# One gather per edge step into fixed buffers, with constant addresses and waits, in both layers of a graph convolution

## The reference

```python
def _gcn_layer(x, src, dst, norm, W, b, num_nodes):
    xw = x @ W
    msg = xw[src] * norm[:, None]          # norm = dis[src] * dis[dst]
    out = segment_sum(msg, dst, num_segments=num_nodes)
    return out + b
...
xn = _layernorm(x)
h = elu(_gcn_layer(xn, ..., W1, b1)); h = elu(_gcn_layer(h, ..., W2, b2))
x = x + h + mix(xn)                        # linear attention, 8 heads
x = x + ffn(_layernorm(x))                 # top 2 of 8 experts, 256 -> 1024 -> 256
```

## Time and profile before

| | us |
|---|---|
| time before, median of 3 runs | 3345.3 |
| lowest and highest of them | 3343.86, 3346.88 |
| span of the profiled execution | 3317.0 |
| PE busy in it | 2369.2 (71%) |
| POOL busy | 1965.4 (59%) |
| DVE busy | 1747.8 (53%) |
| ACT busy | 619.3 (19%) |

### The profile page before, as it was taken

The page is one execution under the profiler, slowest core; times in us unless marked ns, Lnnn a source line. Parts: engine busy times, 40 slices in busy tenths (PEclk is TensorE's granted clock), DMA queues, the critical chain, the costliest instruction groups (busy, mean ns, idle before and its releaser), DMA issues. The chain is left out here.

```text
span 3317.0 us, 45225 instructions
## 1 busy us (share of the span) xinstructions
PE 2369.2 (71%) x10847; PEld 1754.6 (53%) x10847; DVE 1747.8 (53%) x4268; ACT 619.3 (19%) x1318; POOL 1965.4 (59%) x2107
## 2 busy tenths in 40 slices
PE   3366766666776678356666566666669499999998
PEld 2244444444444446234444344434448399999997
DVE  6144444444444456245444455555556666676666
ACT  2000000000000005000000011110006444444443
POOL 1566666666666653766666666666644155555554
PEclk9777888888877879677777877787789599999999
DMA  6333333333333322444444445444431455555551
GB/s 170 114 94 88 93 90 90 92 91 92 89 93 88 89 77 80 122 138 139 141 147 140 140 146 148 146 145 144 144 92 63 170 185 148 148 148 151 148 149 20
DMA packets 177902, 397.25 MB, mean 120 GB/s; under 512 B 42393, under 2 KB 96570, under 8 KB 169514
## 3 DMA queue, kind: packets, MB, share of 16 engines
q0 software_dynamic: 96800, 233.29, 26.7%
q1 hardware_dynamic: 50926, 103.38, 8.7%
q10 hardware_dynamic: 30012, 58.67, 5.2%
HBM read 322.87 MB, written 75.01 MB: 120 GB/s over the span
## 5 line engine op out<-in xcount | busy, mean ns | idle before, releaser
L644 POOL DMA_INDIRECT rows<-rows_layer,srcs x1564 | 1538.3, 984 | 762.3 <-issue 382.0
L705 PE MATMUL l_bank<-rows,sel 128*128 x3332 | 1191.5, 487 | 638.8 <-issue 246.1
L695 DVE TENSOR_TENSOR acc<-acc,l_bank 128x256 f32 x1666 | 698.9, 419 | 1233.1 <-remote 546.7
L705 PEld LDWEIGHTS l_bank<-rows,sel 128*128 128x128 f32 x3332 | 700.3, 235 | 1013.3 <-issue 482.7
L1638 PE MATMUL ps_y<-whl,hhi 128*128 128x512 f32 x896 | 320.8, 398 | 0.0
L1594 POOL DMA_INDIRECT out<-ys,g_sum x112 | 179.9, 1606 | 200.5 <-DVE ys L1550 175.2
L673 DVE TENSOR_TENSOR sel<-iota_n,dloc 128x512 f32<-128x512 f32 x418 | 286.4, 686 | 20.1 <-issue 20.1
L1509 ACT ACTIVATE hr<-ffn_bank,vec 128x256 f32<-128x256 f32 x448 | 212.7, 475 | 374.2 <-PE ffn_bank L1450 336.8
L1448 PE MATMUL ffn_bank<-xh,whl 128*128 128x256 f32 x896 | 252.2, 281 | 2.4 <-DVE xl L1524 2.4
L1449 PE MATMUL ffn_bank<-xl,whl 128*128 128x256 f32 x896 | 252.0, 281 | 0.0
L1450 PE MATMUL ffn_bank<-xh,whl 128*128 128x256 f32 x896 | 251.9, 281 | 0.0
(11 more groups left out here) (273 smaller groups left out, 2208.3 us busy)
## 6 DMA issues: line engine op xcount, KB each, us to landing
whl<-w_hi SPq DMA_DIRECT2D x32, 1024.0 KB
whl<-w_lo SPq DMA_DIRECT2D x32, 1024.0 KB
rows<-rows_layer,srcs POOLq DMA_INDIRECT x1564
w_qkv<-wide ACTq DMA_DIRECT2D x49, 335.0 KB
w_hi<-whi ACTq DMA_DIRECT2D x49, 335.0 KB
w_lo<-wlo ACTq DMA_DIRECT2D x49, 335.0 KB
rows_layer<-acc SPq DMA_DIRECT2D x25, 256.0 KB, 2.1
rows_x<-acc SPq DMA_DIRECT2D x7, 910.0 KB
```

The costliest lines, as they stand in the source:

```text
L644: pool.indirect_dma_start(rows[:, (n + 1) % ROWS, :], None, table[layer], bass.IndirectOffsetOnAxis(ap=srcs[:, n:n + 1], axis=0)).then_inc ...
L695: v.tensor_tensor(to, to, step_bank(s), ALU.add).wait_op(sem(f"summed{layer}"), s + 1, "sem-ge").then_inc(sem(f"added{layer}"), 1)
L705: t.matmul(step_bank(s), sel[:, s % SELS, :], rows_flat[:, bass.ds(slot * D, D)], start=True, stop=True).wait_op(sem(f"here{layer}"), t.to ...
```

## The change

Gathers, matmuls and adds now go by the same number, the step. `srcs` holds an index column for each of the 833 steps instead of 782 tiles, so a tile that two blocks share is gathered twice. Step s writes and reads slot s % 32, PE waits for the landing of its own step by a constant, and POOL waits by a constant for PE's sum 32 steps earlier. `tiles_here`, `steps_until_free` and `tiles_of` go; SP has nothing to do in the layers. DVE's part of a step is unchanged, its register loads (`blocks_of`) too. In the preparation the sources are gathered by `t_i` on POOL like the destinations, seven indirect DMAs behind the seven, in place of SP's two plain ones, and one set of word pairs is stored instead of three.

```diff
-        srcs = sb(steps_ctx, "srcs", [P, ET], I32)
+        srcs = sb(steps_ctx, "srcs", [P, SG * P], I32)
...
-                    sp.wait_ge(sem("copy_s"), 32)
-                    sp.dma_start(rows_i[:, 1, 0:SG - 1, :], e_src_rows[0:full, :].rearrange("(g p) w -> p g w", p=P)
-                                 ).then_inc(sem("rows_s"), 16)
-                    sp.dma_start(rows_i[0:ET - full, 1, SG - 1, :], e_src_rows[full:ET, :]).then_inc(sem("rows_s"), 16)
-                    sp.wait_ge(sem("word_i"), 6)
+                    sp.wait_ge(sem("word_i"), 2)
                     with nc.allow_non_contiguous_dma("small"):
-                        for k in range(3):
-                            sp.dma_start(tab_d[k, :, :].rearrange("(g p) w -> p g w", p=P), word_i[:, k, :, :]
-                                         ).then_inc(sem("word_d"), 16)
+                        sp.dma_start(tab_d[0, :, :].rearrange("(g p) w -> p g w", p=P), word_i[:, :, :]
+                                     ).then_inc(sem("word_d"), 16)
...
                         pool.indirect_dma_start(rows_i[:, 0, g, :], None, e_dst_rows, at).then_inc(sem("rows_d"), 16)
+                    pool.wait_ge(sem("copy_s"), 32)
+                    for g in range(SG):
+                        at = bass.IndirectOffsetOnAxis(ap=t_i[:, g:g + 1], axis=0)
+                        pool.indirect_dma_start(rows_i[:, 1, g, :], None, e_src_rows, at).then_inc(sem("rows_s"), 16)
                     pool.wait_ge(sem("counted"), 2)
...
                     for k in range(2):
-                        v.tensor_scalar(word_i[:, 0, :, k], t_i[:, :], 1.0, None, ALU.add).then_inc(sem("word_i"), 1)
-                        v.tensor_scalar(word_i[:, 1, :, k], b_s[:, :], float(D), None, ALU.mult).then_inc(sem("word_i"), 1)
-                        v.tensor_copy(word_i[:, 2, :, k], tb[:, :]).then_inc(sem("word_i"), 1)
+                        v.tensor_scalar(word_i[:, :, k], b_s[:, :], float(D), None, ALU.mult).then_inc(sem("word_i"), 1)
...
         def gathers(pool, layer, rows):
-            for n in range(ET):
-                if n >= ROWS:
-                    pool.wait_ge(sem(f"freed{layer}"), n - ROWS + 1)
-                pool.indirect_dma_start(rows[:, (n + 1) % ROWS, :], None, table[layer],
-                                        bass.IndirectOffsetOnAxis(ap=srcs[:, n:n + 1], axis=0)
-                                        ).then_inc(sem(f"slot_{n % ROWS}"), 16)
+            for s in range(STEPS):
+                if s >= ROWS:
+                    pool.wait_ge(sem(f"summed{layer}"), s - ROWS + 1)
+                pool.indirect_dma_start(rows[:, s % ROWS, :], None, table[layer],
+                                        bass.IndirectOffsetOnAxis(ap=srcs[:, s:s + 1], axis=0)
+                                        ).then_inc(sem(f"slot_{s % ROWS}"), 16)
+        def landed(layer, s):
+            return (s // ROWS + 1 + layer * -(-(STEPS - s % ROWS) // ROWS)) * 16
...
-        def step_sum(t, layer, s, here):
-            slot = t.snap(here & (ROWS - 1))
-            t.to_reg(slot)
+        def step_sum(t, layer, s, rows):
             if s < PSB:
                 t.wait_ge(sem(f"selected{layer}"), s // FOUR + 1)
             else:
                 t.wait_ge(sem(f"added{layer}"), s - PSB + 1)
-            t.matmul(step_bank(s), sel[:, s % SELS, :], rows_flat[:, bass.ds(slot * D, D)], start=True, stop=True
-                     ).wait_op(sem(f"here{layer}"), t.to_reg(here), "sem-ge").then_inc(sem(f"summed{layer}"), 1)
+            t.matmul(step_bank(s), sel[:, s % SELS, :], rows[:, s % ROWS, :], start=True, stop=True
+                     ).wait_op(sem(f"slot_{s % ROWS}"), landed(layer, s), "sem-ge").then_inc(sem(f"summed{layer}"), 1)
...
-                @block.sync
-                def _(sp):
-                    tiles_here(sp, 0)
```

More of the change, by code:

```diff
@@ L36 @@
 TURN = 16
-BEHIND, FREED_AT = 16, 8
-assert ROWS > BEHIND and ROWS & (ROWS - 1) == 0 and PAD_DST + NT < 1 << 16 and BLOCKS * D < 1 << 16 and ET < 1 << 16
+assert PAD_DST + NT < 1 << 16 and BLOCKS * D < 1 << 16 and ET < 1 << 16
 HEADS, HD = 8, 32
@@ L106, in gps_layer @@
     e_src = dram("edges_src", [ET * P, 1], I32)
-    tab_d = dram("step_words", [3, SG * P, 2], U16)
+    tab_d = dram("step_words", [1, SG * P, 2], U16)
     table = [dram(f"rows_layer{i}", [n * P, D], F32) for i, n in enumerate((NT, 2 * PAIRS))]
@@ L152, in gps_layer @@
         dloc = sb(steps_ctx, "dloc", [P, SG * P])
-        srcs = sb(steps_ctx, "srcs", [P, ET], I32)
-        words = sb(steps_ctx, "words", [3, SG * P, 2], U16)
+        srcs = sb(steps_ctx, "srcs", [P, SG * P], I32)
+        words = sb(steps_ctx, "words", [1, SG * P, 2], U16)
         ctx_q = sb(steps_ctx, "ctx_q", [P, KC, D])
@@ L364, in gps_layer @@
             b_128 = sb(ph, "b_128", [P, SG])
-            word_i = sb(ph, "word_i", [P, 3, SG, 2], U16)
+            word_i = sb(ph, "word_i", [P, SG, 2], U16)
             rows_i = sb(ph, "rows_i", [P, 2, SG, P], I32)
@@ L403, in _ @@
                 def _(sp):
-                    full = ET // P * P
-                    sp.wait_ge(sem("copy_s"), 32)
-                    sp.dma_start(rows_i[:, 1, 0:SG - 1, :], e_src_rows[0:full, :].rearrange("(g p) w -> p g w", p=P)
-                                 ).then_inc(sem("rows_s"), 16)
-                    sp.dma_start(rows_i[0:ET - full, 1, SG - 1, :], e_src_rows[full:ET, :]).then_inc(sem("rows_s"), 16)
-                    sp.wait_ge(sem("word_i"), 6)
+                    sp.wait_ge(sem("word_i"), 2)
                     with nc.allow_non_contiguous_dma("small"):
-                        for k in range(3):
-                            sp.dma_start(tab_d[k, :, :].rearrange("(g p) w -> p g w", p=P), word_i[:, k, :, :]
-                                         ).then_inc(sem("word_d"), 16)
+                        sp.dma_start(tab_d[0, :, :].rearrange("(g p) w -> p g w", p=P), word_i[:, :, :]
+                                     ).then_inc(sem("word_d"), 16)
                     sp.wait_ge(sem("rows_d"), SG * 16)
@@ L418, in _ @@
                     sp.dma_start(node[0:TAIL, NT - 1, :], x[(NT - 1) * P:N, :]).then_inc(sem("x_last"), 16)
-                    sp.wait_ge(sem("word_d"), 48)
+                    sp.wait_ge(sem("word_d"), 16)
                     sp.dma_start(words[:, :, :], tab_d).then_inc(sem("words"), 16)
@@ L571, in _ @@
                             ins.then_inc(sem("rows_t"), 1)
-                    t.wait_ge(sem("rows_f"), 2)
+                    t.wait_ge(sem("rows_f"), 1)
                     for g in range(SG):
-                        n = min(P, ET - g * P)
-                        ins = t.transpose(ps_src[:, g * P:g * P + n], rows_f[0:n, g, :], ident[0:n, 0:n])
+                        ins = t.transpose(ps_src[:, g * P:(g + 1) * P], rows_f[:, g, :], ident[:, :])
                         if g % 4 == 3 or g == SG - 1:
@@ L610, in _ @@
                     a.activation(hi_b[:, :], hi_i[:, :], ACT.Copy).then_inc(sem("hi_b"), 1)
[L611 to L615, removed]
+                    a.wait_ge(sem("rows_s"), SG * 16)
+                    a.activation(rows_f[:, :, :], rows_i[:, 1, :, :], ACT.Copy).then_inc(sem("rows_f"), 1)
+                    for j, (lo, hi) in enumerate(ROW_COLS):
                         a.wait_ge(sem("rows_t"), j + 3)
@@ L679, in blocks_of @@
             _, regs = nc.values_load_multi_w_load_instructions(
-                words[1:2, s:min(s + LOADED, STEPS), 0], engines=(DVE_ENGINE,), min_val=0, max_val=(BLOCKS - 1) * D,
+                words[0:1, s:min(s + LOADED, STEPS), 0], engines=(DVE_ENGINE,), min_val=0, max_val=(BLOCKS - 1) * D,
                 skip_runtime_bounds_check_because="a step's tile is one of the step's number or less, by less than the blocks")
-            return list(regs)
-        def tiles_of(s):
-            _, regs = nc.values_load_multi_w_load_instructions(
-                words[0:1, s:min(s + LOADED, STEPS), 0], engines=(PE_ENGINE,), min_val=1, max_val=ET,
-                skip_runtime_bounds_check_because="a count of tiles, 1 to ET")
             return list(regs)
@@ L720, in vector_steps, with tensor_steps @@
                     between(s // TURN, s % TURN)
-        def tensor_steps(t, layer, between):
-            tiles = tiles_of(0)
+        def tensor_steps(t, layer, rows, between):
             for s in range(STEPS):
-                step_sum(t, layer, s, tiles[s])
-                if s % LOADED == 1 and s + LOADED - 1 < STEPS:
-                    tiles.extend(tiles_of(s + LOADED - 1))
+                step_sum(t, layer, s, rows)
                 if s < NT * TURN:
@@ L741, in gps_layer @@
             rows = sb(ph, "rows0", [P, ROWS, D])
-            rows_flat = rows[:, :, :].rearrange("p r d -> p (r d)")
             sel = sb(ph, "sel0", [P, SELS, P])
@@ L841, in between @@
                             ins.then_inc(sem("m_kv"), 1)
-                    tensor_steps(t, 0, between)
```

(6 more changed lines are left out.)

## The result

The changed kernel takes 3439.1 us (3437.7 to 3440.1, 4 runs) against 3345.5 us, a ratio of 1.0278 with the interval 1.0263 to 1.0292: 93.6 us slower. The forecast was 3420 us, slower by 74.5.

A forecast was written before the change was run, and what follows sets the result against it. PE's late completions after gathers in a row, not POOL's own work, were taken to bound the layers. 2 x (40.8 - 4.9) + 2.7 = +74.5 on 3345.3 gave 3419.8, say 3420 us; range 3162 to 3491.

The forecast's parts named there:

- case A: Whole kernel: the jam stays and 51 more gathers a layer lengthen it, 3382 to 3491 us; chance 0.52.
- the jam: Both layers: after some ten microseconds of gathers in a row, PE's completions come late until POOL pauses.
- The signs: Profile after: 833 gathers 1.39 to 1.45 us apart, POOL idle for PE, layers about 36 us longer, preparation wait near 31.4.
- signs of being wrong: Profile after: gathers 1.29 us apart without waits, a mean gather above 986 ns, or preparation moved over 10 us.
- The base of p: Layer 0 before: gathers start 1.450 us apart in the 3317.0 us span, with 28.3 us lying around it.
- What p becomes: Both layers: gather spacing falls from 1.450 to 1.41 us through PE's lighter step, making +40.8 us a layer.
- The drain: After each layer's last gather: at most 32 steps of 0.786 us remain, 25.2 instead of 30.1 us, -4.9 a layer.
- The preparation: Before layer 0: seven more gathers delay DVE's release from 22.64 to 31.4, costing +2.7 us.
- The bound of -6.1: Preparation: if the gathered destinations land as early as DVE can take them, its 6.11 us idle time goes.
- PE's loads, waits and SP's part at nothing: Layers: PE's register loads and waits and SP's removed work get no term of their own.
- Rival B: Layers: PE's and SP's register and semaphore work causes the jam, so it goes and POOL binds, 3162 us; chance 0.28.
- Case C: Layers: the jam partly eases through PE's lighter step, gathers 1.35 to 1.387 us apart, 3320 to 3382 us; chance 0.20.

The follow-up runs named there:

- run 9: Kernel before, with SP's three word-pair stores moved behind its loads of x: 3336.8 us against 3341.6, ratio 0.9987, on a chip with the jam.
- run 10: Changed kernel fetching 64 rows of 1 KB instead of 128 from each layer's 33rd gather on: 3444.4 us against 3341.6, on a chip with the jam.
- run 8: Changed kernel with three stores of word pairs and their four small DVE operations put back: 3138.5 us, 6.8 above the changed kernel on that chip.
- run 12: Kernel before with the three stores late and a ring of 16 slots, SP 8 tiles behind: 3010.5 us against 3015.1, ratio 0.9985.
- runs 2 and 11: Changed kernel with PE's register loads and operations put back, on two chips without the jam: 3135.9 us (ratio 1.0398) and 3132.9 us (1.0382).
- run 5: Changed kernel as it is, on a chip without the jam: 3131.7 us against 3014.4 for the kernel before, ratio 1.0384.
- run 3: Changed kernel with only the first 32 gathers of each layer, all other work kept: 2474.8 us, on a chip without the jam.
- run 1: Kernel before, unchanged and profiled again, on a chip without the jam: 3016.3 us, with a span of 3014.4.

## Why the prediction was right, and where its steps were off

**The side and the case.** The forecast case A happened: the jam stayed, 51 gathers a layer came on top. The time of 3439 lies inside A's own range. That the price is the number of gathers was shown by leaving 51 of them out (run 6), on a chip without the jam. With the jam it rests on the two traces, which have the same steps and nearly the same price of a gather; no run left gathers out there.

**The signs.** Three of those named came true: 833 gathers a layer, 1.444 us apart, with POOL waiting for PE for 832 x (1.444 - 1.286) = 131 us a layer; DVE's add standing 7.68 us at the end of a run of gathers; and all behind layer 1 as long as it was. Two did not: the layers grew by 63 us and not 36, and DVE's wait in the preparation ended at 22.72 and not near 31.4. And one of the signs of being wrong was touched: the mean of a gather is 987 ns over both layers and 994 in layer 0, where 986 was the bound. That bound divides the window's 771.4 us by 782 gathers where it held 781, which makes 988, and over both layers the gathers before had 984. So this is a few us a layer and not a cause of its own.

**The base of p.** The prediction took 1.450 us a gather from one profiled execution of 3317.0 us and put the 28.3 us up to the median down to what lies around a span. They don't lie there: in every later run the time is 1.7 to 2 us above the span (3439.97 and 3438.2 for the changed kernel). So the profiled execution was some 27 us quicker than the timed ones. Run 9, whose layers are those of the kernel before, has 1.466 and 1.462 us a gather on a chip with the jam. Had the sum started from 1.464, the train of gathers would have been 781 x 1.464 = 1143 us a layer, 11 us longer than the 1132.3 used.

**What p becomes.** Taken was 1.41, measured were 1.444 and 1.443. This is the term that was mis-sized, by 832 x 0.033 = 28 us a layer. The change may have lowered p, from about 1.464 by 0.02 (the 1.464 is run 9's, perhaps from another chip), and not by the 0.04 that the count of PE's instructions gave. The formula, a fixed pause after a run that stretches with PE's lighter step, did not hold: in the cycles shown the run went from 15 gathers to 16, not to 18.75. Run 10 shows that the pauses fill up whatever a gather leaves, so p in the jam isn't a gather's length plus a pause over n.

**Why the time came so close.** In part by luck. The two trains were 1201.6 and 1200.2 us where 1173.1 was taken, +55.6 in all. Against that stand -27.4 (0.9 us between the span and the median instead of 28.3), -7.0 of the preparation and -2.3 of the drains and the rest. That leaves +18.9, and the result stands 19.3 above the 3419.8.

**The drain.** From the end of the last gather to the end of the last add 23.8 us in both layers, before 30.1 and 28.4, in run 9 27.5 and 27.1. Expected were 25.2 after and a gain of 4.9; against run 9 the gain is 3.5. The step was right, the size nearly.

**The preparation.** Expected +2.7, measured -4.3. The step that failed is the reading of the earlier trace rows: DVE's release at 22.64 and the end of seven gathers at 22.66 were a coincidence. With fourteen gathers in a row the release stayed at 22.72; in run 9, with seven that end at 23.01, it came at 24.45; and on chips without the jam it comes at 17.44 and 17.20. It is part of the jam, but not tied to the end of a run of gathers. The bound of -6.1 named the right mechanism, the earlier landing; runs 8, 9 and 12 show that the word stores held it up.

**PE's loads, waits and SP's part at nothing.** Right where POOL binds (runs 2 and 11 against run 5). In the jam only the whole was seen: all of it away gave at most some 0.02 us a gather.

**Rival B** stood on the jam as a product of PE's and SP's register and semaphore work. It is ruled out: the changed kernel has the jam without SP's part and without PE's register work, and the kernel before runs free of it with both, on another chip. Only DVE's register loads stand in every run, so that they have a part isn't excluded. B's kernel would have had to be 183 us faster than before; where POOL does run back to back it is 117 us slower. B's sum for such a layer was sound all the same: 1070.0 us of gathers and some 4 of drain, where run 5 has 1062.7 and 1065.8, and 4.4 and 4.3.

**Case C**, a p between 1.35 and 1.387, did not come either. 5240 recorded instructions fewer moved p by 0.02 at most.

**What stays open** is what the jam is. It comes on some chips and not on others. By the traces DVE goes on up to 20 us and ACT 28 us after PE recorded what they wait for. The jam isn't set by the bytes or rows of a gather (run 10), it doesn't need PE's register work, and behind the layers it was not seen: from the last add of layer 1 to the end are 829.6 us in the first profile and 3014.4 - 2184.9 = 829.5 in run 1, on a chip without it. Whether it needs gathers at all (run 3, nearly without gathers, fell on a chip that has no jam), and whether a smaller ring eases it, wasn't measured where it occurs.

## What to carry to other kernels

Making addresses and waits constant is worth something only on the engine that binds; here it was paid for with 6.5% more of the one instruction that sets the pace (51 gathers on 782), and it lost on both kinds of chip. Before removing work from an engine, count what the removal adds to the others in instructions with a fixed price. And don't take the difference between one profile's span and a median as a fixed amount around it: the profiled execution can be a quicker or slower one than those timed.

## What the runs showed of the hardware

- The same program took 3014 to 3017 us on three chips, 3342 us on a fourth and 3345 us in the first pair. On one chip its times differ by 0.1 to 0.6%. The granted clock was 0.863 in run 1 and 0.827 in the first profile, but the clock isn't the cause of the waits: the changed kernel's layer 0 has 0.77 in both kinds, and POOL's gathers are as long (median over both layers 952 ns in run 1, 949 in the first profile).
- An indirect gather of 128 rows of 1 KB takes POOL 952 ns at the median and a gap of 0.30 us; of 64 rows 908 ns; of 128 rows of 512 bytes 951 ns. If the time goes linearly with the rows, the fixed part is some 0.86 us of it (952 less twice 44 ns), an estimate.
- Three stores of word pairs, of 3.5 KB each, ahead of the landing of seven gathers delayed it by 7 us against one such store (35.3 and 28.17, run 8 and run 5).
